# Self stage rewritten, q stored unnormalised, and 1/rms multiplied onto q by POOL in the attention

## What is computed

```python
q = (x @ wq).reshape(B, L, 16, 128); k = (x @ wk).reshape(B, L, 4, 128); v = ...   # x is layer-normed
q = rms_norm(q, q_norm_w); k = rms_norm(k, k_norm_w)                                # over the 128 of a head
q, k = rope(q), rope(k)
k = concat(k, rms_norm(ctx @ wk_ctx)); v = concat(v, ctx @ wv_ctx)                  # 1601 context rows
x = x + softmax(q @ k.T / sqrt(128) + causal) @ v @ wo                              # 4 q heads share one k head
```

## Time and profile before

| what | value |
|---|---|
| runs (us) | 3104.94, 3102.34, 3104.29; median 3104.29 |
| profiled execution | 3110.86 us, span 3109.0 us, mean PE clock 0.969 |
| self stage | first DVE rotate at 29.07, last copy out ends at 257.64 |
| context stage | first matmul 268.67, last transposes 612.18 |
| attention | first scores at 618.61, last multiply of prob on POOL at 2488.54 |
| one attention group | 58.5 us (SP issues raw_q at 1014.11 and at 1072.62) |

### The profile page before, as it was taken

The page is one execution under the profiler, slowest core; times in us unless marked ns, Lnnn a source line. Parts: engine busy times, 40 slices in busy tenths (PEclk is TensorE's granted clock), DMA queues, the critical chain, the costliest instruction groups (busy, mean ns, idle before and its releaser), DMA issues. The chain is left out here.

```text
span 3109.0 us, 61537 instructions
## 1 busy us (share of the span) xinstructions
PE 2893.1 (93%) x18731; PEld 2456.1 (79%) x18731; DVE 2182.6 (70%) x4617; ACT 2027.7 (65%) x5169; POOL 1597.5 (51%) x2081
## 2 busy tenths in 40 slices
PE   5887999899999999999999999999999977599788
PEld 4665888678888888888888888888888864388755
DVE  7995444567777777777777777777777768756544
ACT  5664666667777777777777777777777647656211
POOL 5884333355555555555555555555555444376132
PEclk9998999999999999999999999999999979899799
DMA  4335666610110110110110110110110010254511
GB/s 133 118 112 177 203 203 203 214 55 33 53 46 33 53 46 33 53 46 34 53 46 33 53 46 33 53 46 33 53 46 33 1 46 1 73 166 131 173 39 28
DMA packets 244462, 236.02 MB, mean 76 GB/s; under 512 B 11654, under 2 KB 224527, under 8 KB 244208
## 3 DMA queue, kind: packets, MB, share of 16 engines
q1 hardware_dynamic: 225552, 212.01, 20.8%
q10 hardware_dynamic: 16448, 15.73, 1.7%
q0 software_dynamic: 2208, 5.12, 0.6%
HBM read 148.93 MB, written 84.80 MB: 75 GB/s over the span
## 5 line engine op out<-in xcount | busy, mean ns | idle before, releaser
L952 ACT ACTIVATE pt_hi<-ps_t 128x512 fp32r<-128x512 f32 (+2 forms) x1024 | 570.0, 557 | 415.1 <-PE ps_t L1185 411.8
L1020 DVE TENSOR_REDUCE piece_max<-ps_s 128x1 f32<-128x512 f32 (+2 forms) x1024 | 631.2, 622 | 260.9 <-PE ps_s L1172 232.9
L1046 DVE TENSOR_TENSOR pt_lo<-ps_t,pt_hi 128x512 fp32r<-128x512 f32 (+2 forms) x1024 | 656.0, 641 | 200.5 <-ACT pt_hi L952 184.0
L1116 POOL TENSOR_SCALAR prob<-prob,inv_sum 128x512 f32<-128x512 f32 (+2 forms) x1024 | 637.1, 642 | 282.1 <-DVE inv_sum L1036 282.1
L940 ACT ACTIVATE prob<-ps_s,neg_max 128x512 f32<-128x512 f32 (+2 forms) x1024 | 648.9, 634 | 92.7 <-DVE neg_max L1027 84.1
L1205 PE MATMUL ps_o<-pt_hi,v_hi 128*128 128x256 f32 (+1 forms) x1856 | 595.7, 321 | 0.0
L1185 PE MATMUL ps_t<-ident,prob 128*128 128x128 f32 (+1 forms) x3712 | 572.0, 272 | 1.4 <-DVE pt_lo L1046 1.3
L1207 PE MATMUL ps_o<-pt_hi,v_lo 128*128 128x256 f32 (+1 forms) x1856 | 523.4, 282 | 0.0
L1206 PE MATMUL ps_o<-pt_lo,v_hi 128*128 128x256 f32 (+1 forms) x1856 | 522.2, 281 | 0.0
L1185 PEld LDWEIGHTS ps_t<-ident,prob 128*128 128x128 f32 (+1 forms) x3712 | 456.6, 140 | 60.0 <-issue 1.7
L1167 PE MATMUL ps_s<-k_hi,q_hi 128*128 128x512 f32 (+2 forms) x1024 | 405.2, 396 | 27.8 <-ACT prob L940 19.6
(11 more groups left out here) (267 smaller groups left out, 5619.9 us busy)
## 6 DMA issues: line engine op xcount, KB each, us to landing
v_scratch<-v_out SPq DMA_DIRECT2D x120, 256.0 KB, 2.5
raw_k<-k_scratch SPq DMA_DIRECT2D x32, 960.0 KB
raw_v<-v_scratch SPq DMA_DIRECT2D x32, 960.0 KB
k_scratch<-k_out SPq DMA_DIRECT2D x104, 256.0 KB, 2.4
q_scratch<-out_t SPq DMA_DIRECT2D x64, 256.0 KB, 2.6
raw_q<-q_scratch SPq DMA_DIRECT2D x32, 512.0 KB
c_raw<-in_ctx_t ACTq DMA_DIRECT2D x52, 256.0 KB, 2.8
raw_t<-in_ctx_t SPq DMA_DIRECT2D x24, 512.0 KB, 4.1
```

The lines of the kernel that those rows point to most:

```text
L952: nc.scalar.activation(pt_hi[keys, k % RING, cols], ps_t[keys, k % 2, cols], ACT.Copy).then_inc(hi_done, 1)
L1020: nc.vector.tensor_reduce(piece_max[:, n % 2, p:p + 1], ps_s[:, p, lo - p * PC:hi - p * PC], AX.X, ALU.max).then_inc(max_ready, 1)
L1046: nc.vector.tensor_tensor(pt_lo[keys, k % RING, cols], ps_t[keys, k % 2, cols], pt_hi[keys, k % RING, cols].bitcast(F32), ALU.subtract).th ...
L1116: nc.gpsimd.tensor_scalar(prob[:, n % PB, lo:hi], prob[:, n % PB, lo:hi], inv_sum[:, n % PB:n % PB + 1], 1.0, ALU.mult, ALU.mult).then_inc ...
```

## The change

1. The first block goes. x comes in four parts, the first ahead of the weights, the rest behind; the tables' loads move to ACT's queue.
2. In the self stage q is not normalised. DVE's turn reads ps_p for q directly, and makes all of by_cos; POOL adds (add_parts). Only k has a root. Of four squares ACT makes two with sums and one plain 256-wide one, which DVE reduces. The sums stay in sq_sum for all 16 tiles. Loops are written out. In each tile the order of turns is q1, k, q2, q3, q4; by_cos, by_sin and roped have four places.
3. The context's weights and first two pairs of tiles are loaded and split within the self stage (high_context, low_context, in tiles 4 to 10), into memory that the attention uses again for pt_hi, pt_lo, o_hi, o_lo and one prob.
4. In the context stage POOL makes 64 roots for q, four per body, one behind each root; in body 18 PE turns them, ACT copies them, SP stores them to r_dram by 16 DMAs. The loops are written out.
5. load_kq has a third DMA, which spreads a row of r_dram over 128 partitions (r_all, 512 KB written). POOL multiplies raw_q in place (scale_q), twice 512 a group; the pieces of k are now split before those of q.

```diff
-                    nc.vector.tensor_tensor(normed[:, j, :].rearrange("p (h d) -> p h d", h=GRP),
-                                            ps_p[:, j, :].rearrange("p (h d) -> p h d", h=GRP),
-                                            rms[:, j, :].unsqueeze(2).to_broadcast([P, GRP, HD]), ALU.mult).then_inc(normed_done, 1)
...
+                def turn(g):
+                    t, j, f = rotated(g)
...
+                    if j == 0:
+                        dve.wait_ge(rms_done, t + 1)
...
+                        made = normed[:, :]
+                    else:
+                        dve.wait_ge(square_done, 3 * (f + 1))
+                        made = ps_p[:, j, :]
+                    if g >= RB:
+                        dve.wait_ge(roped_done, g - RB + 1)
...
+                    for s in range(2):
...
+                        nc.vector.tensor_tensor(dst[:, :, s, :], src[:, :, 1 - s, :],
+                                                sines.unsqueeze(1).to_broadcast([P, GRP, HD // 2]), ALU.mult).then_inc(turned, 1)
+                    nc.vector.tensor_tensor(by_cos[:, g % RB, :].rearrange("p (h d) -> p h d", h=GRP), made.rearrange("p (h d) -> p h d", h=GRP),
+                                            table[:, which, 0, tt, :].unsqueeze(1).to_broadcast([P, GRP, HD]), ALU.mult).then_inc(turned, 1)
...
+                low_w(0)
+                low(0)
+                low_w(1)
+                normalise(1)
+                low_w(3)
+                low_w(4)
+                measure(2)
+                measure(3)
+                low(1)
+                dve.wait_ge(table_ready, 5)
+                sum_squares(0)
+                for n in range(NG):
+                    t = n // GRAN
+                    if n % GRAN == 0 and t + 2 < NT:
+                        normalise(t + 2)
+                    if n % GRAN == 2 and t + 4 < NT:
+                        measure(t + 4)
+                    if n % GRAN == 4 and t + 2 < NT:
+                        low(t + 2)
+                    turn(n)
+                    if n + 1 < NG:
+                        sum_squares(n + 1)
...
+                low_w(5)
+                root_x(2)
+                root_x(3)
+                root_k(0)
+                for n in range(NG):
+                    t = n // GRAN
+                    add_parts(n)
+                    if n % GRAN == 4 and t + 1 < NT:
+                        root_k(t + 1)
+                    if n % GRAN == 2 and t + 4 < NT:
+                        root_x(t + 4)
+                    if n % GRAN == 3 and t in range(5, 5 + C_PIECES + 2):
+                        low_context(t - 5)
...
+def scale_q(pool, gpsimd, it, x, operands):
+
+    raw_q, kq_loaded, r_all, q_scaled = operands[0], operands[3], operands[9], operands[10]
+    pool.wait_ge(kq_loaded, (it + 1) * 48)
+    h = slice(2 * x, 2 * x + 2)
+    gpsimd.tensor_tensor(raw_q[:, h, :].rearrange("p h l -> p (h l)"), raw_q[:, h, :].rearrange("p h l -> p (h l)"),
+                         r_all[:, 2 * x * L:2 * (x + 1) * L], ALU.mult).then_inc(q_scaled, 1)
...
+                        if u in (3, 7) and not last:
+                            for x in range(2):
+                                scale_q(pool, nc.gpsimd, i * BODY_IT + (2 if u == 3 else 3), x, operands)
                         if not (last and u == BODY_U - 1):
                             normalise(i, 2 * u + 3)
```

More of the change, by code:

```diff
@@ L128, in self_projections @@
         squares = sb("squares1", [P, 2, GRP * HD])
[L129 to L135, removed]
+        k_mean = sb("k_mean1", [P, NT, NKV])
+        k_rms = sb("k_rms1", [P, NT, NKV])
+        normed = sb("normed1", [P, NKV * HD])
+        RB = 4
+        by_cos = sb("by_cos", [P, RB, GRP * HD])
+        by_sin = sb("by_sin", [P, RB, GRP * HD])
+        roped = sb("roped", [P, RB, GRP * HD])
         out_t = sb("out_t1", [P, GRAN, GRP, P])
@@ L268, in _ @@
-                body(0, False)
-                with act.Fori(1, LAST) as i:
-                    body(i, False)
-                body(LAST, True)
+                    square(f)
+                for n in range(NG):
+                    if n + LEAD < NG:
+                        square(n + LEAD)
+                    if n % GRAN == 1 and n // GRAN + 2 < NT:
+                        high(n // GRAN + 2)
+                    copy_out(n)
+                    if n % GRAN == 3 and n // GRAN in range(4, 4 + C_PIECES + 2):
+                        high_context(n // GRAN - 4)
@@ L467, in _ @@
-                body(0, False)
-                with pe.Fori(1, LAST) as i:
-                    body(i, False)
-                body(LAST, True)
-def context_projections(nc, ctx_dram, wk_dram, wv_dram, kw_dram, wo_dram, q_dram, k_dram, v_dram, half, ident, casts, consts_loaded, ones_bf, operands):
+                transpose_x(0)
+                project(0)
+                transpose_x(1)
+                for f in range(1, LEAD):
+                    project(f)
+                for n in range(NG):
+                    if n % GRAN == 1 and n // GRAN + 2 < NT:
+                        transpose_x(n // GRAN + 2)
+                    if n + LEAD < NG:
+                        project(n + LEAD)
+                    transposes(n)
@@ L653, in _ @@
                 body(0, False, True)
-                with act.Fori(1, LAST - 2) as i:
+                for i in range(1, LAST - 2):
                     body(i, False, True)
@@ L800, in _ @@
                 body(0, False)
-                with pe.Fori(1, LAST) as i:
+                for i in range(1, LAST):
                     body(i, False)
@@ L1137, in _ @@
                     split_kq(0, 1, x)
+                for x in range(2):
+                    scale_q(pool, nc.gpsimd, 1, x, operands)
                 def body(i, last):
@@ L2580, in program @@
[L2580 to L2586 removed]
+        sq_sum = sb("sq_sum1", [P, NT, GRAN, GRP])
```

610 lines of the change are left out of this document (308 added, 302 removed).

## The result

The changed kernel takes 3080.88 us (median of 4 runs, 3078.56 to 3085.10) and the kernel before 3104.61 beside it (4 runs, 3102.34 to 3106.92). The ratio is 0.9923, 95% interval 0.9911 to 0.9935. The profiled execution has a span of 3080.6 us, against 3109.0.

The account below looks back on a forecast made before the run. DVE was taken to bound the self stage, PE the context stage and attention. Self stage -51.0, gap -7.0, context +1.6 and attention +30 sum to -26.4 us, giving 3078; 8 in 10 range 3045 to 3100.

Parts of the forecast that it names:

- Self stage, the tile: Self-stage loop: a tile takes 11.4 us, bounds 10.8 and 12.6; the whole stage, start and end included, gains 51.0 us.
- milder case of rival 2: Self stage: PSUM operands cost DVE more, 192 reads at 0.065 us adding 12 us; total -14, 3090 us; chance 0.05.
- rival 2: Self stage: a chain between DVE, POOL and PE makes a tile 13 us; total -1, 3103 us; chance 0.10.
- stall over the k root in six tiles: Self-stage tiles with a context piece on POOL: DVE stalls up to 1.2 us for the k root, against 0.3 otherwise.
- DVE (10.9) and PE (10.8) are level: Self stage: work per tile is 10.9 us on DVE and 10.8 on PE, so neither is clearly the slower.
- Self stage, the start: Before the self-stage loop: DVE's loop starts at 20.6 us, 21.2 in effect, against 29.07; bounds 19 and 25.
- The tail: Self stage after the last turn: add 1.27, transposes 1.1, copy 0.6, together 3.0 us; stage ends at 206.6.
- The gap: Between self and context stages: loading and splitting w2 and first context tiles moves earlier, -7.0 us, bounds -5 and -8.
- Context stage: Context stage: +1.6 us, from two transposes (0.3) and a longer wait behind r_all's load (about 1.3); bounds 0 and 6.
- Attention: Attention, units 3 and 7: POOL's multiply delays PE about 1.0 us, 30 times, +30 us; bounds 0 and 75.
- Rival 1: Self stage falls and the attention hides POOL's multiply: total -56.4, 3048 us; chance 0.14.
- Rival 3: Attention, units 3 and 7: the whole 2.54 us falls on PE, 78 instead of 30; total +22, 3126 us; chance 0.06.

Follow-up runs that it names:

- experiment 5: Changed kernel with the five operations making the rope tables moved from POOL to DVE, ahead of its third w_lo: 3083.94 us, ratio 0.9929.
- experiment 8: Changed kernel with POOL's six context pieces split at granule 1 of a tile, ahead of the k root, instead of granule 3: 3077.91 us, ratio 0.9912.
- 6: Changed kernel with ACT taking all four squares of a pair of heads, so DVE loses the reduction: 3080.25 us, ratio 0.9921.
- 7: Changed kernel with v of the self stage made by the high parts alone, low parts' products left out: 3082.33 us, ratio 0.9925.
- 11: Changed kernel with the q multiply behind normalise, context pieces earlier and all four squares on ACT: 3044.9 us, ratio 0.9804.
- experiment 4: Kernel before with nothing but its context stage's loops written out: 3107.78 us beside 3107.86, ratio 0.9998.
- 9: Changed kernel with ps_v declared ahead of ps_k, so the two trade places in PSUM: 3082.48 us in one run.
- experiment 1: Changed kernel with POOL's multiply of q in units 3 and 7 moved behind normalise(2u+3): 3053.39 us, ratio 0.9823.
- experiment 2: Changed kernel with one of the two q multiplies before normalise(2u+3) and one behind: 3052.9 us, ratio 0.9824.
- 3: Changed kernel with a third POOL operation, squaring half of r_all, before normalise(2u+3), and SP's group loop written out: 3141.06 us, ratio 1.0107.
- 10: Changed kernel with the q multiply behind normalise and the context pieces split earlier: 3047.16 us, ratio 0.9814.

## Why the prediction was right where it was, and where it was off

**The sum:** -26.4 forecast, -28.4 between the two spans; by the medians 3078 forecast and 3080.88 measured. That it came so near is in part luck. The self stage gained 6.0 less than forecast, and against that stand 3.2 more in the context stage, 3.7 less lost in the attention, 0.1 in the gap and 0.9 behind the attention.

**Self stage, the tile:** 11.4 us forecast, 11.4 measured. The price of a q granule (1.61, measured 1.59) came from the rows of before, since xt_lo showed what an operand in PSUM costs. The milder case of rival 2, dearer operands in PSUM, is excluded: a by_sin with POOL idle takes 0.42 us alone and 0.76 the pair from SBUF (29.79 in the kernel before) and 0.42 and 0.75 from PSUM (25.23 in experiment 5), and all 128 by_sin of q have a mean of 413 ns. By the Trainium skill (Perfetto Trace Analysis, Optimizing Scalar/DVE Operations), from its 60 and 125 ns, each should cost some 65 ns more than from SBUF, which is an estimate; the trace shows no such step. The rule of the Trainium skill on two SBUF operands (SBUF — State Buffer, Who interferes with whom) held: k's by_sin, beside POOL, have a mean of 576 ns, q's 413. The group rows of the changed kernel, 0 to 210 us (busy, mean ns, idle before):
```profile
L374 DVE TENSOR_TENSOR by_sin<-ps_p,rope_w 128x256 f32<-128x256 f32 x128 | 47.6, 413 | 0.8 <-ACT squares L271 0.8
...
L374 DVE TENSOR_TENSOR by_sin<-normed,rope_w 128x256 f32<-128x256 f32 x32 | 17.2, 576 | 0.5
```
The stall over the k root in six tiles was forecast up to 1.2 us and was 1.0, and experiment 8 shows that it was this. That DVE (10.9) and PE (10.8) are level was near the mark: by 6, 7 and 11 DVE's list takes 11.28 in a tile without a context piece, with some 0.3 of it waiting for xt_hi, and PE's 11.06.

**Self stage, the start:** this step failed, by 5 us. Forecast: DVE's loop from 20.6, 21.2 in effect; measured: its normalise(2) at 25.82 and the first turn at 26.15. Two terms were short. low_w(2) was put at 10.6 and began at 14.63, since ACT's third w_hi started only at 13.50, after 1.91 us of waiting for the weights: with a quarter of x first, the bytes did not come as early as the rate of before had it. The DMA engines moved 219 and 237 GB/s in 6 to 8 and 8 to 10 us, and in the kernel before 368 and 344; why, no run shows. And the four tables with their scaling took 5.4 instead of 3.8: the tables 4.80 instead of 2.54, the scaling 0.62. Two DVE splits with two SBUF operands ran beside them (3.75 for the pair, which is 2.3 alone by the 1.23 of 11.62), and the tables took from 0.73 to 1.72 each. The prediction had reckoned with this loss in the loop and forgotten it at the start. Experiment 5, where single instructions of DVE take longer by about the time that a split on POOL runs, bears it out, and shows that moving the tables doesn't mend it.

**The tail:** 3.0 forecast, 4.3 measured (208.31 to 212.63). The add, one set of transposes and one copy were costed, and each took what it was put at (1.26, 1.08, 0.60). What was left out is the queue: all sets go through one ps_t, so a set waits for the copy of the one before. The last four copies stand 1.86 us apart ((212.03 - 206.44) / 3), while DVE turns a granule in 1.59. PE had stood idle 1.37 us before 205.77, and from 207.1 to 212 the granted clock was 0.50; a set of transposes took 0.63 us ahead of that and 1.09 in it. So the last transposes began at 210.91, where their add had ended at 209.66. The end came at 212.63 instead of 206.6: 5.0 of it from the start (26.15 against the effective 21.2), 1.3 from the tail, -0.2 from the loop.

**The gap:** -7.0 forecast, -7.1 measured.

**Context stage:** +1.6 forecast, -1.6 measured. The longer wait for v_out's store came, 6.42 us after 4.37; most of it was ahead of work that PE had in hand, and PE stood 1.6 us for it. How much of this is r_all's is open: it was 0.4 to 1.8 in the traces of the changed kernels, nothing in the kernel before, and 0.5 in experiment 4, which has no r_all. Against it stood some 3 us from a faster step that I had no row for and whose cause experiments 4 and 9 did not find.

**Attention:** +30 forecast, +26.3 measured. The step itself was right: 0.94 us late in the prediction, 0.97 a group in the trace, 0.79 of PE's wait, 30 times, by the rows of a single group of the kernel before. Experiments 1 to 3 show each part of it: no cost without the delay, none up to 1.27, one for one behind it. The 29 periods between SP's issues of raw_q hold +27.9. Of the rest, -1.9 lies between the first scores and SP's next raw_q (44.50 us before, 42.63 after), and it need not be the change's doing. It goes with the granted clock in the first 20 us of the stage, which differs from execution to execution: in the kept traces the stretch takes 44.5 to 45.3 at 0.60 (the kernel before, 5 and 7), 42.6 to 42.7 at 0.82 to 0.83 (the change, 2 and 8) and 41.4 to 41.8 at 0.87 to 0.88 (1, 3, 6, 9, 10 and 11). The old attention, in experiment 4, had 42.5 at 0.76.

Rival 1 (the multiply is hidden, 3048) fell, but it is what experiment 1 made true by moving two lines. Rival 3 (the whole 2.54 on PE) fell with the wait of 0.79, and experiment 2 shows the room that it denied.

## What to carry to other kernels

When an operation is added to an engine with idle time, look at the one place where it is put: who waits for the next instruction on that engine, and how long before that waiter's start it is ready now. The added time (2.54 us here) less the room (1.6) is the price, and a block's place ahead of or behind that instruction can be worth more (27.5 us) than the whole choice of engine. When two engines come near level, taking work off the slower one gives only the distance to the other (0.21 of 1.65 us a tile here), and off the other nothing; look first for waits that a change of order removes. And compare stages by a period that repeats: where a stage begins or ends moved by some 2 us between executions of the same code.

## What the runs showed of the hardware that was not expected

- A wait of 1.91 us of PE's in a stretch that is otherwise full was followed, in about half of the groups, by some 3 us at half the clock, which cost 1.6 us beside the wait. A wait of 0.79 us was not.
- Six 512-wide matmuls with the same operands' shapes take 1.36 us in one kernel and 1.40 in the other, at a granted clock of 1.00 in both, for v but not for k. Neither the loops' form nor the place in PSUM does it.
- Two SBUF operands on DVE beside POOL cost both: a 1024-wide pair on DVE took 3.75 and 4.54 us beside POOL, where one alone takes 1.23, and a 256-wide operation on POOL 1.2 on average, where half of one of 512 is 0.64. A 256-wide operation on DVE took 2.59 us beside a split on POOL and 0.42 otherwise.
- The same code at the attention's start (the change and 5 to 9, first scores to SP's next raw_q) took 41.8 us with a granted clock of 0.87 or 0.88 in its first 20 us, and 45.3 with one of 0.60.
